# Half-precision halves of the hidden activation taken one chunk later, and the first residual tiles loaded and summed after the fifth slice

## The reference

```python
low = x
for _ in range(2):
    l = dwconv(low, h_filter)[:, ::2]
    h = dwconv(low, g_filter)[:, ::2]
    highs.append(h); low = l
low = linear_attention(low, 16)
for h in reversed(highs):
    low = dwconv(repeat(low, 2), h_synth) + dwconv(repeat(h, 2), g_synth)
x = _layernorm(x + layer_norm(x + low, gamma, beta))
h = silu(x @ wg.T) * (x @ wu.T)        # 512 -> 1536
x = _layernorm(x + h @ wd.T)           # 1536 -> 512
```

## Time and profile before

| | us |
|---|---|
| median of 3 runs | 1320.8 (1317.52, 1320.8, 1321.03) |
| profiled execution, its own time | 1315.63 |
| span of the profiled execution | 1313.8 |
| PE busy | 1248.6 (95%) |
| DVE busy | 980.5 (75%) |
| ACT busy | 684.3 (52%) |
| POOL busy | 373.6 (28%) |
| granted TensorE clock, mean of the span | 0.987 |

### The profile page before, as it was taken

How to read it: one execution, slowest core, us unless ns; L and a number is a source line. 1 busy time by engine, 2 the same in 40 slices (tenths; PEclk the granted TensorE clock), 3 DMA queues, 4 the chain that set the end, 5 groups by cost and what they waited for, 6 DMA issues and landing times.

```text
span 1313.8 us, 19451 instructions
## 1 busy us (share of the span) xinstructions
PE 1248.6 (95%) x6000; PEld 639.7 (49%) x6000; DVE 980.5 (75%) x1921; ACT 684.3 (52%) x1427; POOL 373.6 (28%) x794
## 2 busy tenths in 40 slices
PE   8899899989999999989999999999999999999998
PEld 6778444445444444445544444444444444445443
DVE  7888788968889599884889478955888388945241
ACT  6663563467435763457633664356434663366332
POOL 0303323044132441234330441234131432044101
PEclk9899899999999999999999999999999999999999
DMA  8880610016000230004200130004000410010000
GB/s 267 240 209 25 185 49 33 1 52 222 16 32 8 95 115 16 25 25 137 65 33 1 57 129 18 25 25 152 16 32 8 145 39 32 0 56 9 24 8 32
DMA packets 47269, 87.36 MB, mean 66 GB/s; under 512 B 8400, under 2 KB 24016, under 8 KB 46304
## 3 DMA queue, kind: packets, MB, share of 16 engines
q1 hardware_dynamic: 45472, 81.81, 19.2%
q0 software_dynamic: 1728, 4.72, 2.0%
HBM read 66.04 MB, written 25.19 MB: 69 GB/s over the span
## 4 chain that ended last, share of the span: by engine, by line
PE 31%; DVE 29%; issue 16%; ACT 10%; POOL 6%; DVEq 0%; ACTq 0%; POOLq 0%
DVE s_chan L1189 8%; DVE h_f L1552 6%; PE ps_down L593 6%; PE ps_down L594 6%; PE ps_gate L575 4%; PE ps_gate L576 4%; PE ps_up L576 4%; PE ps_up L575 4%; DVE hid L1558 3%; DVE low L1189 2%; ACT hid L1048 2%; DVE h_mem L1189 2%; ACT junk L839 2%; ACT h_f L1044 2%; DVE x L1331 1%
## 5 line engine op out<-in xcount | busy, mean ns | idle before, releaser
L593 PE MATMUL ps_down<-w,hid 128*128 128x512 f16 x768 | 293.8, 383 | 5.1 <-DVE z L1570 5.1
L575 PE MATMUL ps_gate<-x_hi,w 128*128 128x512 f16 x768 | 292.2, 380 | 5.4 <-ACT h_f L1044 2.6
L575 PE MATMUL ps_up<-x_hi,w 128*128 128x512 f16 x768 | 291.7, 380 | 3.3 <-DVE h_f L1552 3.3
L594 PE MATMUL ps_down<-w,hid 128*128 128x512 f16 x768 | 293.4, 382 | 0.0
L576 PE MATMUL ps_gate<-x_lo,w 128*128 128x512 f16 x768 | 292.1, 380 | 0.0
L576 PE MATMUL ps_up<-x_lo,w 128*128 128x512 f16 x768 | 291.6, 380 | 0.0
L1048 ACT ACTIVATE hid<-h_f 128x512 f16<-128x512 f32 x192 | 120.8, 629 | 241.3 <-DVE h_f L1552 241.3
L1552 DVE SCALAR_TENSOR_TENSOR h_f<-ps_up,h_f 128x512 f32<-128x512 f32 x192 | 131.8, 686 | 114.5 <-ACT h_f L1044 84.9
L1558 DVE TENSOR_TENSOR hid<-h_f,hid 128x512 f16<-128x512 f32 x192 | 138.7, 722 | 58.1 <-ACT hid L1048 57.3
L575 PEld LDWEIGHTS ps_up<-x_hi,w 128*128 128x128 f16 x768 | 75.3, 98 | 97.0 <-DVE h_f L1552 6.8
L593 PEld LDWEIGHTS ps_down<-w,hid 128*128 128x128 f16 x768 | 75.7, 99 | 94.0 <-issue 6.3
(11 more groups left out here) (249 smaller groups left out, 1868.1 us busy)
## 6 DMA issues: line engine op xcount, KB each, us to landing
xt<-x_tok SPq DMA_DIRECT2D x64, 256.0 KB, 2.7
out<-z SPq DMA_DIRECT2D x64, 256.0 KB, 2.0
xa<-x_chan SPq DMA_DIRECT2D x28, 515.0 KB, 5.7
xb<-x_chan SPq DMA_DIRECT2D x7, 2060.0 KB, 8.2
w<-weights POOLq DMA_DIRECT2D x12, 384.0 KB, 8.7
q_in<-q_scratch SPq DMA_DIRECT2D x7, 518.0 KB, 8.2
h_in<-h_scratch SPq DMA_DIRECT2D x7, 518.0 KB, 9.2
h_scratch<-h SPq DMA_DIRECT2D x7, 512.0 KB, 9.8
```

The source lines that it names most:

```text
L575: pe.matmul(ps_gu[k % 2][g][:, :], w, x1_hi[:, b, c, :], start=(c == 0), stop=False)
L593: pe.matmul(ps_d[t % 2][:, :], h_hi[:, k, t * P:(t + 1) * P], w, start=(k == 0), stop=False)
L594: mm = pe.matmul(ps_d[t % 2][:, :], h_lo[:, k, t * P:(t + 1) * P], w, start=False, stop=(k == NH - 1))
```

## The change

Two things are done, and no computation is added or removed.

1. In the main loop the high half of chunk k-1 is taken by ACT right after the silu of chunk k, and the low half of chunk k-1 by DVE right after MUL of chunk k. Those of the last chunk (k = 11) follow in the same chunk: on DVE right behind the low half of chunk 10, on ACT behind the early steps.
2. In the opening, SP issues the loads of the first four `xt` tiles behind the last loads of slice a = 4, and POOL adds beta to them behind its last four weight pieces. POOL's third pair of weight loads then follows the second with nothing between that takes time.

```diff
-                if a == 1:
+                if a == PER_BATCH:
                     for t in range(4):
                         load_xt(0, t)
...
+            def high_half(B, k):
+                act.wait_ge(h_mul, NH * B + k + 3)
+                nc.scalar.activation(h_hi[:, k, :], h_f[:, k % RING, :], ACT.Copy).then_inc(hi_done, 1)
...
                                              scale=WSCALE / X1_SCALE).then_inc(silu_done, 1)
+                        if k > 0:
+                            high_half(B, k - 1)
                         beside(b, k, i, batch, analysis, last, early)
-                        act.wait_ge(h_mul, NH * B + k + 3)
-                        nc.scalar.activation(h_hi[:, k, :], h_f[:, k % RING, :], ACT.Copy).then_inc(hi_done, 1)
+                        if k == NH - 1:
+                            high_half(B, k)
                         beside(b, k, i, batch, analysis, last, late)
...
             hold(pool, pro_conv1, 2)
             load_weights(0, 2)
-            pool.wait_ge(ld_const, 96)
-            for t in range(DSUB):
-                xbeta(0, 0, t)
             hold(pool, pro_conv1, 4)
             load_weights(2, 2)
...
             load_weights(8, 4)
+            pool.wait_ge(ld_const, 96)
+            for t in range(DSUB):
+                xbeta(0, 0, t)
             for name, t in CLOSE_POOL:
...
+            def low_half(B, k):
+                dve.wait_ge(hi_done, NH * B + k + 1)
+                V.tensor_tensor(h_lo[:, k, :], h_f[:, k % RING, :], h_hi[:, k, :], ALU.subtract
+                                ).then_inc(lo_done, 1)
...
                                                op0=ALU.mult, op1=ALU.mult).then_inc(h_mul, 1)
+                        if k > 0:
+                            low_half(B, k - 1)
                         if 0 < k < NH - 1:
                             beside(b, k, i, batch, analysis, last, steps)
-                        dve.wait_ge(hi_done, n + 1)
-                        V.tensor_tensor(h_lo[:, k, :], h_f[:, k % RING, :], h_hi[:, k, :], ALU.subtract
-                                        ).then_inc(lo_done, 1)
                         if k == NH - 1:
-
+                            low_half(B, k)
                             beside(b, k, i, batch, analysis, last, steps)
```

## The result

The changed kernel takes **1299.5 us** (median of 4 runs, 1296.8 to 1299.9) against 1320.9 for the kernel before (4 runs): ratio 0.983, 95% interval 0.980 to 0.987, a gain of 21.4 us. A later set of 4 runs gave 1299.4. The direction was right; the gain that was forecast, 9.7 us, is less than half of the measured one.

What follows compares the result with a forecast made beforehand. PE was taken as the bound, busy 95% of the span, so only its waits count. Analysing iterations 9.3, iterations 3 to 6 0.4 and opening 0 make 9.7 us off the median 1320.8: 1311.1 us, range 1302 to 1319.

Steps and rivals of the forecast that it cites:

- the first halves of iterations 3 to 6: Main loop: the moved low half delays silu 8 by 0.95 us, gate 10 waits about 1.0, each half 0.5 us longer.
- the second halves: Iterations 3 to 6: the chain through DVE's norm, POOL and ACT gives 0.6 us back in each second half.
- the prediction's own sign: Main loop: the forecast is wrong if iterations 4 to 6 change by more than 1 us each.
- Analysing iterations: Iterations 0 to 2: first half gains 2.1 us, second 1.0, so 3.1 an iteration and 9.3 for the three.
- the end chain: Second half of analysing iterations: copy releasing PE at 426.31 comes 0.95 us earlier, x_lo releasing it at 437.73 1.05 earlier.
- The opening: Before the main loop: slice 3 starts 2.6 us earlier only; net 0 taken, between 4.0 gained and 2 lost.
- the case that the prediction feared: Opening, slice 2: the 1.2 GHz stretch moves to 40 us, the convolution takes 3 us more, the gain is gone.
- Both bounds: Opening: early weight pieces 2 and 3 delay the xa load by nothing or by their whole 4.4 us; the whole taken.
- "0 to 2": Close of the opening: DVE work meeting a sum may wait, PE has 2 us to spare, so 0 to 2 us lost.
- The sum against the median: Whole kernel: the 9.7 us gained on the 1313.8 us span is taken from the median, 1320.8, giving 1311.1.
- "the opening gains too": Opening rival, chance 0.15: pieces don't delay xa, slice 3 starts 4 or more us earlier; time 1306.
- "Slower": Main loop rival, chance 0.09: low half ahead of the norm costs 1.6 us in each of seven iterations; 1328.

Runs made afterwards that it cites:

- the execution with the sums held: Changed kernel, but POOL holds its four sums with beta until DVE has done the attention products of the opening's close: 1298.8 us, 0.982 of the kernel before.

## Why the prediction was wrong

**The failing step is the first halves of iterations 3 to 6.** "The low half of the former chunk now lies in this loop: it is hit at chunks 2 and 7 ... I find silu 8 0.95 us later, a new wait of about 1.0 us at 933.60, and the z sum 0.5 late at the end of the half ..." For the low half's move alone the mechanism is right, and so are two of the three sizes: silu 8 is 1.02 us later and gate 10 1.0, the z sum 0.9. But the sum had only this term. The late high half frees the same loop at the same time. By itself it does this: ACT no longer stands for MUL of chunk 5, silu 6 comes 2.2 us earlier (25.3 instead of 27.5 us into the half), DVE's wait of 0.49 us for it goes, and MUL 6 with the row sum behind it comes 1.1 us earlier. The prediction had counted just this wait, in the analysing iterations (0.50 for the silu of chunk 6), and dropped it where "the first half is not late on DVE at its start". DVE's wait of 0.70 us for the high half of chunk 11 goes as well. In the changed kernel silu 8 is 0.15 us earlier, no wait appears at gate 10, DVE doesn't wait for the high half of chunk 11, and the z sum comes 0.94 us earlier where 0.5 later was forecast, so that PE's wait of 0.7 us for it is gone. That is 1.4 us a half, 5.7 in all; the second halves gave 0.4 more than forecast each, 1.5 in all. (The waits of PE there, "about 3.5" us an iteration in the prediction, add to 2.9 to 3.0; nothing was worked out from it.) By the prediction's own sign, iterations 4 to 6 changing by more than 1 us, it is wrong: they changed by 1.9 to 2.0.

**Analysing iterations.** The first halves gained 1.8, 2.5 and 2.5 us (forecast 2.1), for the reasons given; the wait for copies at 318.95 grew from 1.40 to 2.17, by 0.8 where 1.1 was forecast. The second halves gained 0.9, 2.0 and 2.3 (forecast 1.0). In iteration 1 most of the excess is the stretch at 1.2 GHz that is missing: with late high halves, executions with such a stretch in that half took 74.0 to 74.3 us for it, those without 73.1 (72.5 in one). The stretches move from run to run, and the forecast had no term for them. With a stretch in both kernels that half gains 0.8 to 1.1 us, the forecast 1.0; so the x_lo that releases PE 2.0 us earlier, not 1.05, doesn't show that the term of the end chain was too small. In iteration 2 both kernels have a stretch and the gain is 2.3; how much of it is the chain and how much the place of the stretch stays open.

**The opening.** Slice 3 starts at 49.4, 5.4 us earlier, not 2.6. The pieces delayed the xa load by 2.3 us, from a landing at 36.1 to 38.4, about half of the 4.4 that was taken for the whole; PE waited 1.26 us there, and no stretch at 1.2 GHz came with it in this execution. With the same opening code up to there, the execution with the sums held had the stretch, from 40.6 to 44.0, and started slice 3 at 51.6, 3.2 us earlier than before: the case that the prediction feared does occur. Both bounds were named, and the upper one was taken where half of it was measured. The Trainium skill (DMA: Bandwidth & Descriptors, "Queues, rings and completion order") has the engines take turns between queues; a delay of part of the pieces' time fits that. The lead of 5.4 us was then lost step by step: the store of slice 4's keys is issued 3.9 us earlier but lands only 1.7 earlier, the copy that needs it starts 1.6 earlier, PE's attention product 0.2 later, and the loop 3.6 later. So the close cost more than the "0 to 2": the "2 us to spare" of PE assumed that the sums start when POOL is free; they start when xt has landed, at 90.2, on top of the filters. And that the store of slice 4's keys bounds the close was not seen at all, though it stood in the trace of before (issued 78.1, landed 89.8).

**The sum against the median.** The prediction set the traced execution 5.2 us below the median and carried the difference unchanged. That difference was most likely the opening's spread: the one other trace of the old opening starts the loop 7.8 us later with a main loop that agrees, so the changed opening had something to gain there, 3.5 us by the medians of that part alone. By medians, loop 18.9 and opening 3.5 make 22.4, against 21.4 and 23.9 measured for both.

**Of the rivals**, "the opening gains too" had the right sign by medians and slice 3 earlier by more than 4, but not for its reason, since the pieces did delay xa; and none had the larger gain of the loop. "Slower" names a loss that exists: with the high half as before, the low half's move costs 3.6 us of main loop, where 7 were forecast. 0.9 us is lost in each first half of iterations 3 to 6 and less than 0.5 in those before; the second halves of iterations 3 to 6 give 0.1 to 0.3 back, and those of iterations 1 and 2 differ by +1.2 and -1.4 with the places of the stretches at 1.2 GHz.

Not settled: what decides whether the old opening runs fast or slow, beyond the order in which the last stores and pieces are issued, and where the stretches at 1.2 GHz fall.

## What to carry to other kernels

When one edit moves two instructions through the same loop, price each alone and then both: here they were -1.1 and +1.0 us at the same silu, and the one that was left out was the gain. A load that nobody needs yet can still be the bound, by what it stands beside: ask of each late store which transfers were issued just before it. And one trace of a program whose runs spread by 10 us is one draw: before its opening is summed to a tenth, look at the spread.

## What the hardware showed

- A DVE instruction with two SBUF inputs behind a row sum holds POOL's one-column multiply from 0.19 to 0.44 or 0.57 us, until DVE's instruction ends; with one input in PSUM it doesn't (0.19).
- One POOL multiply of one column, 0.19 us elsewhere, lasts 2.63 us beside a train of DVE's filters; it was not served between two of them. That is one row, and times on POOL are rough. The other way round, three filters of 0.88 us took 3.10, and three of 1.27 took 4.30, beside POOL's sums.
- Four weight pieces (1.57 MB) in POOL's queue doubled the landing time of a 512 KB store in SP's queue, 7.0 to 13.9 us (13.7 to 14.1 in eight traces).
